# Half-height matmuls for one product of the GNN's first layer, and its bias moved from TensorE to ScalarE

## The chip, the cores and the metric

One core of a Trainium2 chip runs the kernel. The metric is the device time of one execution in microseconds (us), the median over runs. A profile of one further execution shows what each engine did: TensorE (PE, with its weight loads as PEld), VectorE (DVE), ScalarE (ACT), GpSimd (POOL) and SyncE (SP), which issues most DMAs.

## The reference

```
h   = relu(layernorm(x))                        # x: 50000 x 256
agg = mean of edge_attr over the edges by dst   # 25000 x 64 -> 50000 x 64, edges sorted by dst
h1  = relu(concat([agg, h], 1) @ W1 + b1)       # W1: 320 x 512
out = x + (h1 @ W2 + b2)                        # W2: 512 x 256
```

All in fp32.

## The kernel before

**Tiles.** The 50000 rows are worked off in 98 tiles (steps t = 0 to 97) of 512 rows. The hidden width of 512 is cut into CH = 4 chunks m of 128, the output rows of a tile into SUB = 4 groups j of 128. Every fp32 operand X of a matmul is split into a rounded high part X_hi (type fp32r) and the rest X_lo = X - X_hi, and a product is made of three fp32r matmuls: hi by hi, lo by hi, hi by lo.

**Layer 1.** For chunk m, `layer1_nodes` adds six 512-column matmuls into PSUM bank m (two halves c of the node features by three products, lines L795 to L797). `layer1_means` adds two: L804 takes the weights wa_hi (rows of W1 that belong to the means, twice) by QA, whose upper 64 partitions hold the means' high part and whose other 64 hold their low part; L805 takes wb_lo by QB. QB holds the means' high part in partitions 0 to 63 and ones below; wb_lo holds the low weights of the means in partitions 0 to 63 and, in rows 64 and 96, the bias b1 as high and low part against those ones. So L805 does two things with one matmul: the product of the means' high part with the low weights (64 rows), and the bias. Eight matmuls make a chunk, the eighth releases it (s_l1).

**Evictions.** ACT (`hidden_high`, L530) writes H1_hi = relu(bank) as fp32r; then DVE (`hidden_low`, L646) writes H1_lo = max(bank, 0) - H1_hi from the bank and H1_hi.

**Layer 2.** `layer2` makes 16 pairs of a 512-column matmul (L815, H1_hi by both parts of W2) and a 256-column one (L817, H1_lo by W2's high part). Its order is (j0: m0, m1, m2), (j1: m0, m1, m2), (j0: m3), (j1: m3), then j2 and j3 whole. Before each matmul of j0 it waits for H1_lo of that chunk, since the pair needs it. The first six pairs are therefore what TensorE can do between the end of layer 1 and the arrival of H1_lo of chunk 3.

**Order on each engine, written out by hand.**

- TensorE, step t: chunk 0, chunk 1, `edge_means(t+1)` (eight small matmuls of 64 output columns, L784 and L785, that sum edges into the bank PA), chunk 2, chunk 3, layer 2.
- VectorE, step t: H1_lo chunk 0, two statistics, H1_lo chunk 1, two statistics, H1_lo chunk 2, `ends` (L581) and `aggregate` (L589), transpose 0 of tile t+1 (L630), H1_lo chunk 3, transpose 1, the two HT_lo of t+1 (L638), the one-hot matrices of t+2, residual 0 (two instructions), the means' low part of t+1 (`means_low`, L642), residuals 1 to 3.
- ScalarE, step t: H1_hi of chunks 0 to 3, HT_hi of t+1 (two, L516), `means_high(t+1)` (QB L521, QA L523), four layernorm activations of t+2 (HN, L504), E_hi of t+2.
- SP, step t: load of X for t+3, the edge windows of t+3, `move(t+2)` (four DMAs HQ<-HN, L252, once the four layernorm activations are done), the store of t. The transpose of step t+1 reads HQ.

Banks 2 and 3 of layer 1 are also the output banks j = 2 and 3 of layer 2, so layer 1 waits there for residuals of the tile before (s_fin).

Of the kernel before, what the change touches and what calls it, by code (L numbers as in the profile page):

```python
# [20 lines left out]
def past(eng, sem, value):  # L21

    if not isinstance(value, int) or value > 0:
        eng.wait_ge(sem, value)


def build(nc, x, src, dst, edge_attr, w1, b1, w2, b2, out):
    N, D = x.shape
    E, DE = edge_attr.shape
    H = w1.shape[1]  # L30
    CD, CH = D // P, H // P
# [36 lines left out]
    with ExitStack() as ctx:  # L68
        def sb(name, shape, dt=F32):
            return ctx.enter_context(nc.sbuf_tensor(name, shape, dt))  # L70

        def ps(name, shape, dt=F32):
            return ctx.enter_context(nc.psum_tensor(name, shape, dt))

        def sem(name):
            return ctx.enter_context(nc.semaphore(name))


        ident = sb("ident", [P, P])
# [7 lines left out]
        b2_row = sb("b2_row", [P, D])  # L87
        w1_raw = sb("w1_raw", [P, CD, H])
        wa_raw = sb("wa_raw", [P, H])
        b1_raw = sb("b1_raw", [P, H])  # L90
        w2_raw = sb("w2_raw", [P, CH, D])
        w1_hi = sb("w1_hi", [P, CD, H], F32R)
        w1_lo = sb("w1_lo", [P, CD, H], F32R)
        wa_hi = sb("wa_hi", [P, H], F32R)
        wb_lo = sb("wb_lo", [P, H], F32R)
        b1_hi = sb("b1_hi", [P, H], F32R)
        w2_both = sb("w2_both", [P, CH, 2, D], F32R)


# [43 lines left out]
        HT_hi = sb("HT_hi", [P, CD, TILE], F32R)  # L143
        HT_lo = sb("HT_lo", [P, CD, TILE], F32R)
        QA = sb("QA", [P, TILE], F32R)
        QB = sb("QB", [P, TILE], F32R)
        H1_hi = sb("H1_hi", [P, CH, TILE], F32R)
        H1_lo = sb("H1_lo", [P, CH, TILE], F32R)

# [23 lines left out]
        PA = ps("PA", [P, TILE])  # L173
# [177 lines left out]
        @block.gpsimd  # L351
        def _(pool):
            pool.memset(dst_b[:], 1 << 20).then_inc(s_zero, 1)
            pool.memset(b1_raw[:], 0.0).then_inc(s_zero, 1)
            pool.iota(thresholds[:], pattern=[[P, KS], [TILE, TILES]], base=0, channel_multiplier=0,
                      allow_small_or_imprecise_dtypes=True).then_inc(s_zero, 1)
            pool.wait_ge(s_zero, 3)
            pool.iota(thresholds[:, :, TILES - 1:TILES], pattern=[[P, KS], [0, 1]], base=LAST, channel_multiplier=0,
                      allow_small_or_imprecise_dtypes=True).then_inc(s_const, 1)
            pool.memset(ones_bf[:], 1.0).then_inc(s_const, 1)  # L360
# [55 lines left out]
            pool.wait_ge(s_whi, 5)  # L416
# [68 lines left out]
        def _(act):  # L485
# [3 lines left out]
                              w1[DE + q * QF:DE + (q + 1) * QF, :].rearrange("(c f) h -> f c h", f=QP)).then_inc(s_w[0], 16)  # L489
            for a in range(2):  # L490
                act.dma_start(wa_raw[a * DE:(a + 1) * DE, :], w1[0:DE, :]).then_inc(s_w[1], 16)
            act.wait_ge(s_zero, 3)
            for p in (64, 96):
                act.dma_start(b1_raw[p:p + 1, :], b1.rearrange("(o h) -> o h", o=1)).then_inc(s_w[2], 16)
            for a in range(2):
                act.dma_start(w2_raw[:, 2 * a:2 * a + 2, :],
                              w2[2 * a * P:2 * (a + 1) * P, :].rearrange("(c p) d -> p c d", p=P)).then_inc(s_w[3], 16)
# [20 lines left out]
            def means_high(t):  # L518
                past(act, s_l1, CH * t)
                act.wait_ge(s_sum, t + 1)  # L520
                act.activation(QB[0:DE, :], PA[0:DE, :], ACT.Copy).then_inc(s_qhi, 1)  # L521
                act.wait_ge(s_qhi, 2 * t + 1)
                act.activation(QA[0:DE, :], QB[0:DE, :], ACT.Copy).then_inc(s_qhi, 1)  # L523

            def hidden_high(t):
                for m in range(CH):
                    act.wait_ge(s_l1, CH * t + m + 1)
                    if m == 0:
                        past(act, s_l2, SUB * t)
                    act.activation(H1_hi[:, m, :], bank(m)[:], ACT.Relu).then_inc(s_1hi, 1)  # L530

            act.wait_ge(s_w[0], 16 * QN)
            act.activation(w1_hi[:], w1_raw[:], ACT.Copy).then_inc(s_whi, 1)
            act.wait_ge(s_w[1], 32)
            act.activation(wa_hi[:], wa_raw[:], ACT.Copy).then_inc(s_whi, 1)
            act.wait_ge(s_w[2], 32)
            act.activation(b1_hi[DE:P, :], b1_raw[DE:P, :], ACT.Copy).then_inc(s_whi, 1)
            act.activation(wb_lo[64:96, :], b1_raw[64:96, :], ACT.Copy).then_inc(s_whi, 1)
            act.wait_ge(s_w[3], 32)
            act.activation(w2_both[:, :, 0, :], w2_raw[:], ACT.Copy).then_inc(s_whi, 1)  # L540
            layernorm(0, 0)
# [27 lines left out]
        def _(dve):  # L569
# [69 lines left out]

            def means_low(t):  # L640
                dve.wait_ge(s_qhi, 2 * t + 1)
                dve.tensor_tensor(QA[DE:P, :], PA[0:DE, :], QB[0:DE, :], ALU.subtract).then_inc(s_qlo, 1)  # L642

            def hidden_low(t, m):
                dve.wait_ge(s_1hi, CH * t + m + 1)
                dve.scalar_tensor_tensor(out=H1_lo[:, m, :], in0=bank(m)[:], scalar=0.0, in1=H1_hi[:, m, :],  # L646
                                         op0=ALU.max, op1=ALU.subtract).then_inc(s_1lo, 1)

            def residual(t, b, j):
                dve.wait_ge(s_l2, SUB * t + j + 1)  # L650
# [8 lines left out]
            def step(t, b, later=True, latest=True):  # L659
# [22 lines left out]
                for j in range(1, SUB):  # L682
# [13 lines left out]
                                     in1=behind[:, HALO:HALO + ER_], op0=ALU.add, op1=ALU.add).then_inc(s_runs, 1)  # L696
# [6 lines left out]
            with dve.If(flag != 0):  # L703
# [3 lines left out]
                with dve.Fori(0, SLOTS) as i:  # L707
# [40 lines left out]
            ends(0, 0)  # L748
            onehot(0, 0)

            dve.wait_ge(s_whi, 3)
            dve.tensor_tensor(wb_lo[0:DE, :], wa_raw[0:DE, :], wa_hi[0:DE, :], ALU.subtract).then_inc(s_wblo, 1)
            dve.tensor_tensor(wb_lo[96:P, :], b1_raw[96:P, :], b1_hi[96:P, :], ALU.subtract).then_inc(s_wblo, 1)
            means_low(0)
            ends(1, 1)
            onehot(1, 1)
# [10 lines left out]
        def _(pe):  # L767
# [7 lines left out]
            pe.wait_ge(s_const, 13)  # L775

            def edge_means(t, b):
                pe.wait_ge(s_oh, SUB * t + SUB)
# [9 lines left out]
            def layer1_nodes(t, m):  # L788
                if m == 0:
                    pe.wait_ge(s_hlo, 2 * t + 2)  # L790
                if m >= 2:
                    past(pe, s_fin, SUB * (t - 1) + m + 1)
                cols = slice(m * P, (m + 1) * P)
                for c in range(CD):
                    pe.matmul(bank(m)[:], w1_hi[:, c, cols], HT_hi[:, c, :], start=(c == 0), stop=False)  # L795
                    pe.matmul(bank(m)[:], w1_hi[:, c, cols], HT_lo[:, c, :], start=False, stop=False)  # L796
                    pe.matmul(bank(m)[:], w1_lo[:, c, cols], HT_hi[:, c, :], start=False, stop=False)  # L797

            def layer1_means(t, m):
# [78 lines left out]
```

## Time and profile before

| | |
|---|---|
| median of 3 runs | 1381.35 us (1381.05 to 1381.44) |
| the profiled execution | 1381.12 us |
| its span from the first to the last instruction | 1379.1 us |
| mean granted TensorE clock | 0.989 |
| busy: PE, PEld, DVE, ACT, POOL | 1340.5, 1122.1, 1202.3, 696.5, 533.0 us |

A matmul's record lasts from its start to the modelled end of its results, so records of consecutive matmuls overlap; what a matmul costs is the distance from its start to the next one's. Between steps the pattern repeats every 13.54 us.

### The profile page before, as it was taken

The numbers are of one execution on the slowest core, as the hardware profiler recorded it, in microseconds if no ns is written. First come the engines' busy times: TensorE is split into PE (matmuls) and PEld (weight loads), VectorE is DVE, ScalarE is ACT, GpSimd is POOL, SyncE is SP. The second block draws the span as 40 slices with busy tenths as digits, with TensorE's granted clock in tenths as the row PEclk, the third lists the DMA queues.
The fourth block names the chain that finished last, engine by engine and source line by source line (L and its number), as shares of the span: only waits on it lengthen the run. The fifth ranks groups of instructions, "written<-read, shape, count | busy, mean of one in ns | idle before, by whom it ended". The sixth has DMA issues, their size and how long they took to land.

```text
span 1379.1 us, 29845 instructions
## 1 busy us (share of the span) xinstructions
PE 1340.5 (97%) x7078; PEld 1122.1 (81%) x7078; DVE 1202.3 (87%) x2979; ACT 696.5 (51%) x1280; POOL 533.0 (39%) x709
## 2 busy tenths in 40 slices
PE   2799999999999999999999999999999999999998
PEld 0588888888888888888888888888888888888887
DVE  7598989898888989898988888898889898898986
ACT  3354545455554545454555545454545555454543
POOL 4334343433333343434333343434343443434341
PEclk7899999999999999999999999999999999999999
DMA  5567676766767676867667676758676766767672
GB/s 108 89 122 136 115 143 110 138 113 135 116 132 129 119 138 113 143 111 138 114 135 115 133 131 117 133 118 142 109 141 113 136 117 131 120 129 132 118 128 56
DMA packets 424904, 169.49 MB, mean 123 GB/s; under 512 B 323190, under 2 KB 424506, under 8 KB 424892
## 3 DMA queue, kind: packets, MB, share of 16 engines
q1 hardware_dynamic: 421608, 167.40, 67.0%
q10 hardware_dynamic: 3284, 1.97, 0.8%
q14 instruction: 9, 0.07, 0.0%
q8 instruction: 3, 0.05, 0.0%
HBM read 66.50 MB, written 51.40 MB: 85 GB/s over the span
## 4 chain that ended last, share of the span: by engine, by line
PE 96%; DVE 2%; DMA 1%; SPq 1%; issue 0%
PE P L815 26%; PE P L817 14%; PE P L795 13%; PE P L797 13%; PE P L796 13%; PE P L804 7%; PE P L805 7%; PE PA L785 2%; PE PA L784 2%; DVE below L597 1%; DMA X<-in_x_dram 0%; DMA dst_a<-in_dst_dram 0%; SPq L275 0%; DMA table_dram<-table 0%; SPq L276 0%
## 5 line engine op out<-in xcount | busy, mean ns | idle before, releaser
L815 PE MATMUL P<-w_both,H_hi 128*128 128x512 f32 x1568 | 552.1, 393 | 4.7 <-DVE H_lo L646 4.7
L530 ACT ACTIVATE H_hi<-P 128x512 fp32r<-128x512 f32 x392 | 234.6, 599 | 509.9 <-PE P L805 509.9
L817 PE MATMUL P<-w_both,H_lo 128*128 128x256 f32 x1568 | 442.5, 282 | 0.0
L646 DVE SCALAR_TENSOR_TENSOR H_lo<-P,H_hi 128x512 fp32r<-128x512 f32 x392 | 268.8, 686 | 108.4 <-ACT H_hi L530 101.8
L815 PEld LDWEIGHTS P<-w_both,H_hi 128*128 128x128 f32 x1568 | 295.3, 188 | 71.0 <-DVE H_lo L646 6.2
L795 PE MATMUL P<-HT_hi,w_hi 128*128 128x512 f32 x784 | 316.0, 403 | 19.5 <-DVE HT_lo L638 19.5
L797 PE MATMUL P<-HT_hi,w_lo 128*128 128x512 f32 x784 | 310.8, 396 | 0.0
L796 PE MATMUL P<-HT_lo,w_hi 128*128 128x512 f32 x784 | 310.4, 396 | 0.0
L817 PEld LDWEIGHTS P<-w_both,H_lo 128*128 128x128 f32 x1568 | 297.0, 189 | 4.5
L409 POOL TENSOR_TENSOR XB<-X,b_row 128x1024 f32<-128x1024 f32 x98 | 234.9, 2397 | 137.9 <-DVE O L657 137.9
L403 POOL TENSOR_TENSOR E_lo<-ES,E_hi 128x256 fp32r<-128x256 f32 x98 | 73.1, 746 | 416.0 <-ACT E_hi L510 416.0
L630 DVE STREAM_TRANSPOSE HT<-HQ 128x512 f32<-128x512 f32 x196 | 212.9, 1087 | 7.3 <-DMA HQ<-HN 5.7
L504 ACT ACTIVATE HN<-X,shift,rstd 128x256 f32<-128x256 f32 x392 | 202.4, 587 | 10.2 <-POOL shift L392 10.2
L795 PEld LDWEIGHTS P<-HT_hi,w_hi 128*128 128x128 f32 x784 | 148.1, 189 | 49.7 <-issue 19.6
L516 ACT ACTIVATE HT_hi<-HT 128x512 fp32r<-128x512 f32 x196 | 123.9, 633 | 127.2 <-DVE HT L630 127.1
L657 DVE TENSOR_TENSOR O<-P,XB 128x256 f32<-128x256 f32 x392 | 166.5, 425 | 13.4
L797 PEld LDWEIGHTS P<-HT_hi,w_lo 128*128 128x128 f32 x784 | 147.8, 189 | 35.3
L796 PEld LDWEIGHTS P<-HT_lo,w_hi 128*128 128x128 f32 x784 | 148.2, 189 | 26.4
L655 DVE TENSOR_TENSOR XB<-P,XB 128x256 f32<-128x256 f32 x392 | 163.9, 418 | 4.7 <-PE P L817 1.6
L804 PE MATMUL P<-QA,wa_hi 128*128 128x512 f32 x392 | 155.1, 396 | 1.6 <-DVE QA L642 1.6
L805 PE MATMUL P<-QB,wb_lo 128*128 128x512 f32 x392 | 154.1, 393 | 0.0
L638 DVE TENSOR_TENSOR HT_lo<-HT,HT_hi 128x512 fp32r<-128x512 f32 x196 | 134.6, 687 | 17.9 <-ACT HT_hi L516 16.1
(72 smaller groups left out, 1136.9 us busy)
## 6 DMA issues: line engine op xcount, KB each, us to landing
X<-in_x_dram SPq DMA_DIRECT2D x98, 512.0 KB, 4.2
HQ<-HN SPq DMA_DIRECT2D x388, 128.0 KB, 4.2
out_dram<-O SPq DMA_DIRECT2D x97, 512.0 KB, 4.8
ER<-in_edge_attr_dram SPq DMA_DIRECT2D x392, 32.0 KB, 1.8
DT<-table_dram SPq DMA_DIRECT2D x392, 1.0 KB, 1.7
w_raw<-in_L_gnn_W_dram ACTq DMA_DIRECT2D x4, 128.0 KB, 7.2
w_raw<-in_L_gnn_W_dram ACTq DMA_DIRECT2D x2, 256.0 KB, 8.6
HQ<-HN ACTq DMA_DIRECT2D x4, 128.0 KB, 4.1
```

The source lines that it names most:

```text
L409: pool.tensor_tensor(XB[b][:], X[b][:], b2_row[:].unsqueeze(1).to_broadcast([P, SUB, D]), ALU.add).then_inc(s_xb, 1)
L504: act.activation(HN[b][:, j, :], X[b][:, j, :], ACT.Relu, bias=shift[b][:, j:j + 1], scale=rstd[b][:, j:j + 1]).then_inc(s_ln, 1)
L530: act.activation(H1_hi[:, m, :], bank(m)[:], ACT.Relu).then_inc(s_1hi, 1)
L630: dve.transpose(HT[:, c, :].rearrange("p (j n k) -> p k j n", j=SUB, k=QN), HQ[b][:, :, c * QP:(c + 1) * QP].rearrange("p (k j) f -> p k j ...
L646: dve.scalar_tensor_tensor(out=H1_lo[:, m, :], in0=bank(m)[:], scalar=0.0, in1=H1_hi[:, m, :], op0=ALU.max, op1=ALU.subtract).then_inc(s_1 ...
L795: pe.matmul(bank(m)[:], w1_hi[:, c, cols], HT_hi[:, c, :], start=(c == 0), stop=False)
L796: pe.matmul(bank(m)[:], w1_hi[:, c, cols], HT_lo[:, c, :], start=False, stop=False)
L797: pe.matmul(bank(m)[:], w1_lo[:, c, cols], HT_hi[:, c, :], start=False, stop=False)
L804: pe.matmul(bank(m)[:], wa_hi[:, cols], QA[:], start=False, stop=False)
L805: pe.matmul(bank(m)[:], wb_lo[:, cols], QB[:], start=False, stop=True).then_inc(s_l1, 1)
L815: pe.matmul(out_bank(j)[:], H1_hi[:, m, rows], w2_both[:, m, :, :].rearrange("p a d -> p (a d)"), start=(m == 0), stop=False)
L817: last = pe.matmul(out_bank(j)[:, 0:D], H1_lo[:, m, rows], w2_both[:, m, 0, :], start=False, stop=(m == CH - 1))
```

## The change

The bias leaves the matmuls. The product of the means' high part with the low weights becomes matmuls of 64 rows: the one for chunk m reads partitions 0 to 63 (QA, wb_lo), the one for chunk m+1 reads partitions 64 to 127 (QC, a second copy of the high part, and the second copy of the low weights in wb_lo). The two follow each other at the head of chunks 0 and 2 and write different banks. `layer1_means` keeps one matmul per chunk. ScalarE adds the bias, now a column b1_col per chunk, in two evictions of each chunk: H1_hi in fp32r as before, and H1 in fp32. VectorE subtracts the two, both from SBUF, instead of reading the bank.

```
-        b1_raw = sb("b1_raw", [P, H])
+        b1_col = sb("b1_col", [P, CH])
-        QB = sb("QB", [P, TILE], F32R)
+        QC = sb("QC", [P, TILE], F32R)
+        H1 = sb("H1", [P, CH, TILE])
 # gpsimd: memsets of b1_raw and of QB's ones are gone
 # scalar, start
-            act.wait_ge(s_zero, 3)
-            for p in (64, 96):
-                act.dma_start(b1_raw[p:p + 1, :], b1.rearrange("(o h) -> o h", o=1)).then_inc(s_w[2], 16)
+            act.dma_start(b1_col[:], b1.rearrange("(m p) -> p m", p=P),
+                          allow_slow_non_contiguous=True).then_inc(s_w[2], 16)
-            act.activation(b1_hi[DE:P, :], b1_raw[DE:P, :], ACT.Copy).then_inc(s_whi, 1)
-            act.activation(wb_lo[64:96, :], b1_raw[64:96, :], ACT.Copy).then_inc(s_whi, 1)
 # scalar, means_high
-                act.activation(QB[0:DE, :], PA[0:DE, :], ACT.Copy).then_inc(s_qhi, 1)
+                act.activation(QA[0:DE, :], PA[0:DE, :], ACT.Copy).then_inc(s_qhi, 1)
                 act.wait_ge(s_qhi, 2 * t + 1)
-                act.activation(QA[0:DE, :], QB[0:DE, :], ACT.Copy).then_inc(s_qhi, 1)
+                act.activation(QC[DE:P, :], QA[0:DE, :], ACT.Copy).then_inc(s_qhi, 1)
 # scalar, hidden_high
-                    act.activation(H1_hi[:, m, :], bank(m)[:], ACT.Relu).then_inc(s_1hi, 1)
+                    act.activation(H1_hi[:, m, :], bank(m)[:], ACT.Relu, bias=b1_col[:, m:m + 1]).then_inc(s_1hi, 1)
+                    act.activation(H1[:, m, :], bank(m)[:], ACT.Relu, bias=b1_col[:, m:m + 1]).then_inc(s_1, 1)
 # vector
-                dve.tensor_tensor(QA[DE:P, :], PA[0:DE, :], QB[0:DE, :], ALU.subtract).then_inc(s_qlo, 1)
+                dve.tensor_tensor(QA[DE:P, :], PA[0:DE, :], QA[0:DE, :], ALU.subtract).then_inc(s_qlo, 1)
                 dve.wait_ge(s_1hi, CH * t + m + 1)
-                dve.scalar_tensor_tensor(out=H1_lo[:, m, :], in0=bank(m)[:], scalar=0.0, in1=H1_hi[:, m, :],
-                                         op0=ALU.max, op1=ALU.subtract).then_inc(s_1lo, 1)
+                dve.wait_ge(s_1, CH * t + m + 1)
+                dve.tensor_tensor(H1_lo[:, m, :], H1[:, m, :], H1_hi[:, m, :], ALU.subtract).then_inc(s_1lo, 1)
 # tensor
-                if m >= 2:
-                    past(pe, s_fin, SUB * (t - 1) + m + 1)
+            def layer1_pair(t, m):
+                first = not (isinstance(t, int) and t == 0)
+                if m == 0:
+                    pe.wait_ge(s_qhi, 2 * t + 2)
+                else:
+                    past(pe, s_fin, SUB * t)
+                pe.matmul(bank(m)[:], wb_lo[0:DE, m * P:(m + 1) * P], QA[0:DE, :], start=first, stop=False)
+                pe.matmul(bank(m + 1)[:], wb_lo[DE:P, (m + 1) * P:(m + 2) * P], QC[DE:P, :], start=first, stop=False)
 # tensor, layer1_means
-                pe.matmul(bank(m)[:], wa_hi[:, cols], QA[:], start=False, stop=False)
-                pe.matmul(bank(m)[:], wb_lo[:, cols], QB[:], start=False, stop=True).then_inc(s_l1, 1)
+                pe.matmul(bank(m)[:], wa_hi[:, m * P:(m + 1) * P], QA[:], start=False, stop=True).then_inc(s_l1, 1)
 # tensor, step
                 for m in range(CH):
+                    if m % 2 == 0:
+                        layer1_pair(t, m)
                     if not (isinstance(t, int) and t == 0):
                         layer1_nodes(t, m)
                     layer1_means(t, m)
```

## Rows read from the trace of the kernel before

**Rows 1.** The page's head, and its part on busy time.

```profile
span 1379.1 us, 29845 instructions
...
PE 1340.5 (97%) x7078; PEld 1122.1 (81%) x7078; DVE 1202.3 (87%) x2979; ACT 696.5 (51%) x1280; POOL 533.0 (39%) x709
```

**Rows 2.** The page's chain that ended last, by engine.

```profile
PE 96%; DVE 2%; DMA 1%; SPq 1%; issue 0%
```

**Rows 3.** The page's groups: the two evictions' lines.

```profile
L530 ACT ACTIVATE H_hi<-P 128x512 fp32r<-128x512 f32 x392 | 234.6, 599 | 509.9 <-PE P L805 509.9
...
L646 DVE SCALAR_TENSOR_TENSOR H_lo<-P,H_hi 128x512 fp32r<-128x512 f32 x392 | 268.8, 686 | 108.4 <-ACT H_hi L530 101.8
```

**Rows 4.** Timeline, one step, TensorE: start, length, engine, line, operation.

```profile
702.03 0.22 PE L785 MATMUL PA<-OH,E_lo 128*64 128x128 f32 x1
702.03 0.19 PEld L795 LDWEIGHTS P<-HT_hi,w_hi 128*128 128x128 f32 x1
702.09 0.45 PE L795 MATMUL P<-HT_hi,w_hi 128*128 128x512 f32 x1
...
702.37 0.40 PE L796 MATMUL P<-HT_lo,w_hi 128*128 128x512 f32 x1
...
703.77 0.39 PE L805 MATMUL P<-QB,wb_lo 128*128 128x512 f32 x1
...
705.86 0.40 PE L815 MATMUL P<-w_both,H_hi 128*128 128x512 f32 x1
...
706.10 0.28 PE L817 MATMUL P<-w_both,H_lo 128*128 128x256 f32 x1
...
707.96 0.39 PE L815 MATMUL P<-w_both,H_hi 128*128 128x512 f32 x1
...
711.31 0.28 PE L817 MATMUL P<-w_both,H_lo 128*128 128x256 f32 x1
...
711.43 0.40 PE L795 MATMUL P<-HT_hi,w_hi 128*128 128x512 f32 x1
```

**Rows 5.** Timeline, the same step, ScalarE, VectorE and SP's queue.

```profile
701.10 0.69 DVE L646 SCALAR_TENSOR_TENSOR H_lo<-P,H_hi 128x512 fp32r<-128x512 f32 x1
...
704.20 0.60 ACT L530 ACTIVATE H_hi<-P 128x512 fp32r<-128x512 f32 x1 [1.79 <-PE P L805]
...
704.82 0.69 DVE L646 SCALAR_TENSOR_TENSOR H_lo<-P,H_hi 128x512 fp32r<-128x512 f32 x1 [1.03 <-ACT H_hi L530]
...
705.81 1.11 DVE L630 STREAM_TRANSPOSE HT<-HQ 128x512 f32<-128x512 f32 x1
...
706.75 0.68 DVE L646 SCALAR_TENSOR_TENSOR H_lo<-P,H_hi 128x512 fp32r<-128x512 f32 x1
...
709.62 0.63 ACT L523 ACTIVATE QA<-QB 64x512 fp32r<-64x512 f32 x1
...
710.16 2.07 ACT L504 ACTIVATE HN<-X,shift,rstd 128x256 f32<-128x256 f32 x4
...
712.25 2.73 SPq L252 DMA_DIRECT2D HQ<-HN  x4
```

**Rows 6.** Timeline, first step: two evictions in a row, and X's arrival.

```profile
45.83 1.06 ACT L530 ACTIVATE H_hi<-P 128x512 fp32r<-128x512 f32 x2
...
52.45 0.75 DVE L575 BATCH_NORM_STATS2 stats<-X 128x6 f32<-128x256 f32 x2 [5.32 <-DMA X<-in_x_dram]
```

**Rows 7.** Timeline, a later step in which TensorE waited inside layer 2.

```profile
883.39 0.67 DVE L646 SCALAR_TENSOR_TENSOR H_lo<-P,H_hi 128x512 fp32r<-128x512 f32 x1
...
883.86 0.28 PE L817 MATMUL P<-w_both,H_lo 128*128 128x256 f32 x1
...
884.11 0.51 PE L815 MATMUL P<-w_both,H_hi 128*128 128x512 f32 x1
...
884.45 0.28 PE L817 MATMUL P<-w_both,H_lo 128*128 128x256 f32 x1
```

**Rows 8.** The tile HQ, whole run: waits for it (us, times); its DMAs.

```profile
  DMA HQ<-HN: 5.7, 23
...
DMA to landing us min/median/max: 3.3/4.2/5.4
```

More of the change, by code:

```diff
@@ L95, in build @@
         wb_lo = sb("wb_lo", [P, H], F32R)
-        b1_hi = sb("b1_hi", [P, H], F32R)
         w2_both = sb("w2_both", [P, CH, 2, D], F32R)
@@ L226, in build @@
         s_1hi = sem("s_1hi")
+        s_1 = sem("s_1")
         s_1lo = sem("s_1lo")
@@ L353, in _ @@
             pool.memset(dst_b[:], 1 << 20).then_inc(s_zero, 1)
-            pool.memset(b1_raw[:], 0.0).then_inc(s_zero, 1)
             pool.iota(thresholds[:], pattern=[[P, KS], [TILE, TILES]], base=0, channel_multiplier=0,
                       allow_small_or_imprecise_dtypes=True).then_inc(s_zero, 1)
-            pool.wait_ge(s_zero, 3)
+            pool.wait_ge(s_zero, 2)
             pool.iota(thresholds[:, :, TILES - 1:TILES], pattern=[[P, KS], [0, 1]], base=LAST, channel_multiplier=0,
@@ L375, in _ @@
             pool.wait_ge(s_const, 10)
-            pool.memset(QB[DE:P, :].bitcast(F32), 1.0).then_inc(s_const, 1)
+            pool.memset(ident[:], 0.0).then_inc(s_const, 1)
             pool.wait_ge(s_const, 11)
-            pool.memset(ident[:], 0.0).then_inc(s_const, 1)
-            pool.wait_ge(s_const, 12)
             pool.affine_select(out=ident[:], in_=ident[:], compare_op=ALU.not_equal, fill=1.0, base=0,
@@ L415, in _ @@
             pool.tensor_tensor(w1_lo[:], w1_raw[:], w1_hi[:], ALU.subtract).then_inc(s_wlo, 1)
-            pool.wait_ge(s_whi, 5)
+            pool.wait_ge(s_whi, 3)
             pool.tensor_tensor(w2_both[:, :, 1, :], w2_raw[:], w2_both[:, :, 0, :], ALU.subtract).then_inc(s_wlo, 1)
@@ L535, in _ @@
             act.activation(wa_hi[:], wa_raw[:], ACT.Copy).then_inc(s_whi, 1)
-            act.wait_ge(s_w[2], 32)
-            act.activation(b1_hi[DE:P, :], b1_raw[DE:P, :], ACT.Copy).then_inc(s_whi, 1)
-            act.activation(wb_lo[64:96, :], b1_raw[64:96, :], ACT.Copy).then_inc(s_whi, 1)
+            act.wait_ge(s_w[2], 16)
             act.wait_ge(s_w[3], 32)
@@ L749, in _ @@
             onehot(0, 0)
-            dve.wait_ge(s_whi, 3)
-            dve.tensor_tensor(wb_lo[0:DE, :], wa_raw[0:DE, :], wa_hi[0:DE, :], ALU.subtract).then_inc(s_wblo, 1)
-            dve.tensor_tensor(wb_lo[96:P, :], b1_raw[96:P, :], b1_hi[96:P, :], ALU.subtract).then_inc(s_wblo, 1)
+            dve.wait_ge(s_whi, 2)
+            dve.tensor_tensor(wb_lo[:], wa_raw[:], wa_hi[:], ALU.subtract).then_inc(s_wblo, 1)
             means_low(0)
@@ L774, in _ @@
             pe.matmul(PA[0:1, 0:1], ones_f[0:EP, :], fall[:], start=True, stop=True).then_inc(s_found, 1)
-            pe.wait_ge(s_const, 13)
+            pe.wait_ge(s_const, 12)
             def edge_means(t, b):
@@ L790, in layer1_nodes @@
                     pe.wait_ge(s_hlo, 2 * t + 2)
-                if m >= 2:
-                    past(pe, s_fin, SUB * (t - 1) + m + 1)
                 cols = slice(m * P, (m + 1) * P)
                 for c in range(CD):
-                    pe.matmul(bank(m)[:], w1_hi[:, c, cols], HT_hi[:, c, :], start=(c == 0), stop=False)
+                    pe.matmul(bank(m)[:], w1_hi[:, c, cols], HT_hi[:, c, :],
+                              start=(c == 0 and isinstance(t, int) and t == 0), stop=False)
                     pe.matmul(bank(m)[:], w1_hi[:, c, cols], HT_lo[:, c, :], start=False, stop=False)
                     pe.matmul(bank(m)[:], w1_lo[:, c, cols], HT_hi[:, c, :], start=False, stop=False)
+            def layer1_pair(t, m):
[6 more added lines that the diff above has]
+                pe.matmul(bank(m + 1)[:], wb_lo[DE:P, (m + 1) * P:(m + 2) * P], QC[DE:P, :], start=first, stop=False)
             def layer1_means(t, m):
@@ L801, in layer1_means @@
                     pe.wait_ge(s_qlo, t + 1)
-                    pe.wait_ge(s_qhi, 2 * t + 2)
-                cols = slice(m * P, (m + 1) * P)
-                pe.matmul(bank(m)[:], wa_hi[:, cols], QA[:], start=False, stop=False)
-                pe.matmul(bank(m)[:], wb_lo[:, cols], QB[:], start=False, stop=True).then_inc(s_l1, 1)
+                pe.matmul(bank(m)[:], wa_hi[:, m * P:(m + 1) * P], QA[:], start=False, stop=True).then_inc(s_l1, 1)
             def layer2(t):
@@ L846, in _ @@
             pe.wait_ge(s_wlo, 2)
-            pe.wait_ge(s_wblo, 2)
-            pe.wait_ge(s_whi, 5)
+            pe.wait_ge(s_wblo, 1)
+            pe.wait_ge(s_whi, 3)
             step(0, 0)
```

## The prediction

> **What bounds the kernel now.** I read the page's busy times first, then the chain that ended last, then one step of the timeline. TensorE is busy for 97% of the span and is 96% of the chain [rows 1, 2]; VectorE follows with 87%, ScalarE is at 51%. A share doesn't tell whether TensorE could go faster, so the timeline of one step matters. There the first L795 of a step starts 13.54 us after the one before (the pattern's period), and the matmuls stand without a gap: six pairs of layer 2 take 707.96 - 705.86 = 2.10 us, 0.35 each, of which the 512-column matmul is 0.233 (705.86 to 706.10) and the 256-column one 0.116 [rows 4]. So a period is 32 layer-1 matmuls x 0.233 = 7.45, plus 16 x 0.35 = 5.58, plus about 0.5 for the eight edge matmuls: TensorE is filled. Any matmul taken out is worth its 0.233 us, as long as nothing else comes due. The rest of this prediction is about what comes due.
>
> The nearest thing is H1_lo of chunk 3. The seventh L815 (707.96) needs it; DVE ended it at 706.75 + 0.68 = 707.43 [rows 4, 5]. The slack is 0.53 us.
>
> **The change, part by part.** All times below are per step, in us.
>
> *Taken out:* four full L805, 4 x 0.233 = 0.93.
>
> *Added on TensorE:* two pairs of 64-row matmuls of 512 columns. No row shows a 64-row matmul. The bounds: if the two run at the same time, a pair costs one matmul, 0.24; if they run one after the other, 0.466; either may have a cost of switching on top. Between them lies the weight load. Both pairs stand behind a short matmul: the first behind a 256-column L817, the second behind the last 128-column L785 [rows 4]. A load starts when the matmul before starts; after the last L785 the load of L795 started at 702.03, and the next matmul came at 702.37 and not 0.233 after 702.09, so the full load took until about 702.14, or 0.11. If the second load of a pair can't go together with the first, the second matmul starts 0.11 late and a pair costs 0.35. I take 0.24: the halves use different partitions, different weights and different banks, so nothing that I see has to be shared. TensorE's work is then 13.54 - 0.93 + 0.48 = 13.09.
>
> The Trainium skill, page "TensorE: Matmul & The Clock Gate", Part 3 (The mechanism), has such matmuls start some 4 ns apart, with the loads pulled ahead; that would make a pair 0.24, and the sum above stands at it. No row here shows it.
>
> *Added on ScalarE:* a second eviction per chunk. Two evictions in a row took 1.06 together, so the second starts 0.46 after the first and ends 1.06 after the first's start [rows 6]; a bias from another address should not change this. ScalarE has 509.9 us of idle time before its evictions [rows 3], over five a step, and takes four times 0.46 = 1.84 more: not a bound. But the low part now waits for the second eviction: it comes 0.46 later behind its chunk.
>
> *VectorE:* subtracts from SBUF and no longer from the bank. I take the same 0.69 as for L646 [rows 3]; no gain, no loss.
>
> *The new wait.* Let S be the start of the last matmul of chunk 2 (703.77, L805). Before: eviction at S + 0.43, H1_lo of chunk 2 at S + 1.05, transpose 0 at 705.81, which is 0.99 behind it, H1_lo of chunk 3 at 706.75, another 0.94, and its end 0.68 later: S + 3.66 [rows 4, 5]. The eviction of chunk 3 is not what this waits for; VectorE's order is. After: everything from H1_lo of chunk 2 on is 0.46 later, so its chunk 3 ends at S + 4.12. TensorE gets there sooner: chunk 3 has seven matmuls instead of eight, so the seventh L815 comes due at S + 0.233 x 8 + 2.10 = S + 3.96 (before S + 4.19). It is late by 0.16. On top comes what a wait costs when it happens: in the one example H1_lo ended at 883.39 + 0.67 = 884.06, the L815 was recorded at 884.11, and the L817 behind it came 0.34 after that and not 0.233, because its weight load was no longer hidden [rows 7]. So 0.16 after the end of H1_lo the matmul really runs. The stall is 0.16 + 0.16 = 0.32.
>
> *What is late behind it.* Transpose 1, HT_hi, the means, the layernorm and the HQ moves hang on transpose 0 and shift along. Between transpose 0 and the end of the layernorm activations lie 712.23 - 705.81 = 6.42; from there to the next transpose 0 there are 13.54 - 6.42 = 7.12 for four DMAs, whose last is issued some 2.1 after and landed up to 5.4 later [rows 5, 8]. Today this wait occurs 23 times for 5.7 us in all, and mostly disappears in the slack of 0.53. With a period near 13.41 the room shrinks by 0.13, and there is no slack in front of TensorE any more: (5.7 + 23 x 0.13) / 97 = 0.09; I take 0.08.
>
> *Things that I cost at nothing.* The pair needs QC at the head of the step: the copy ended at 709.62 + 0.63 = 710.25 [rows 5], 5.43 behind H1_lo of chunk 2. In the new step, counted from the start of its first pair, S is at 0.24 + 14 x 0.233 + 0.53 + 0.24 + 6 x 0.233 = 5.67, that H1_lo at 7.18, QC at 12.6, and the next pair at 13.4: 0.8 to spare. The pair of chunk 2 waits for all four residuals of the step before instead of three: these were done when the next step's first H1_lo started, 701.10 + 13.54 - 704.82 = 9.82 behind that of chunk 2, so at 17.0, and the pair comes at 13.4 + 4.0 = 17.4: 0.4 to spare. If either cover went, TensorE would stall by the excess in every step. The start (bias load, two activations, a subtraction and two memsets fewer) ends in any case with the wait for X until 52.45 [rows 6].
>
> *Sum.* 13.09 + 0.32 + 0.08 = 13.49, against 13.54. 96 steps save 0.05, 4.8 us, and the last step, which has no transpose in front of its H1_lo, saves the full 0.45. 1381.12 - 5.2 = 1375.9. The profiled execution is 0.2 below the median of 1381.35, so I say 1376. Of 44 us that TensorE's own work gives up (97 x 0.45), nearly all is eaten by the later low part.
>
> **The rivals.**
>
> *A, my forecast (chance 0.45):* pairs at 0.24. 1376; with the stall 0.1 smaller or larger it is 1366 to 1386.
>
> *B, the second weight load shows (0.25):* a pair is 0.35, TensorE's work 13.31, with the stall 0.32 and a little HQ wait (0.03) 13.66, 0.12 more than now: 1392. Slower. It decides from the point where the pair exceeds 0.27. For it: both pairs stand behind short matmuls [rows 4]. Against it: the loads use different rows.
>
> *C, no side by side at all (0.15):* four matmuls of 0.233 as before, so only the later low part counts: 13.54 + 0.32 + 0.03 = 13.89, 0.35 more: 1381 + 34 = 1415. For it: no row shows two matmuls at once.
>
> *D, the array empties at each change of height (0.10):* a matmul's record is 0.39 long and the next starts after 0.233 [rows 4], so emptying costs up to 0.16; four changes per step are 0.64. 13.49 + 0.64 - 0.05 = 14.08: 1381 + 52 = 1433. Against it: the change to the edge matmuls' 64 columns and back costs only 0.05 (702.09 to 702.37 is 0.28) [rows 4].
>
> The Trainium skill, page "TensorEngine Tiling (Array Packing)", Key Properties, has a change of tiling mode drain TensorE; that is this case. The 0.05 around the edge matmuls, a change of columns, speaks against it; a change of rows no run has shown so far.
>
> *E, the stall doesn't come (0.05):* were H1_lo of chunk 3 on time, only TensorE's work would count: 13.09, 97 x 0.45 = 44 less, 1338. The 0.16 by which it is late leaves little room for that.
>
> **How the numbers follow.** The likeliest is A, 1376, with 1366 to 1386 of its own. The range leaves out D and the depth of E: 1364 to 1416. What tells a change from none here is 0.2%, 2.8 us: below 1378.6 lies some two thirds of A and all of E, 0.36; between 1378.6 and 1384.1 some of A and a bit of B, 0.14; above, the rest of A, B, C and D, 0.50.
>
> **What would show it.** The two L-lines of the pair should start a few ns apart, and the matmul behind them 0.24 after the first (B: 0.35; C: 0.47). Before the seventh L815 of a step there should be idle time ended by H1_lo, some 0.2 us by the record, in nearly every step, and the L817 behind it at 0.34. ScalarE should be near 64% to 65% busy. DVE's idle time before H1_lo, now 108.4 us, should rise, and the waits for HQ be more than 23. I am wrong if pairs don't overlap, if a bias from a table of its own makes the eviction longer, or if the subtraction from SBUF takes another time than that from PSUM.

## The result, and the profile after

The changed kernel takes 1490.34 us (median of 4 runs, 1490.01 to 1491.79) against 1381.39 us before: a ratio of 1.0788 (95% interval 1.0773 to 1.0803). It is 109 us slower. The forecast was 1376 us with a range of 1364 to 1416; even the worst rival, 1433, was too fast.

The page of the changed kernel: span, busy times, the chain by engine, and the groups of the evictions and of GpSimd's addition.

```profile
span 1487.1 us, 30480 instructions
...
PE 1419.4 (95%) x7078; PEld 1089.3 (73%) x7078; DVE 1388.1 (93%) x2978; ACT 967.1 (65%) x1670; POOL 531.6 (36%) x707
...
PE 51%; DVE 21%; issue 19%; ACT 5%; DVEq 2%; SPq 1%; DMA 1%; POOL 0%; POOLq 0%
...
L643 DVE TENSOR_TENSOR H_lo<-H,H_hi 128x512 fp32r<-128x512 f32 x392 | 466.8, 1191 | 38.9 <-ACT H L528 38.9
L527 ACT ACTIVATE H_hi<-P,b_col 128x512 fp32r<-128x512 f32 x392 | 269.7, 688 | 299.8 <-PE P L806 299.8
...
L407 POOL TENSOR_TENSOR XB<-X,b_row 128x1024 f32<-128x1024 f32 x98 | 234.4, 2391 | 125.5 <-DVE O L653 125.5
L528 ACT ACTIVATE H<-P,b_col 128x512 f32<-128x512 f32 x392 | 267.2, 682 | 0.0
```

Against [rows 1 to 3]: TensorE was 96% of the chain and is 51%; VectorE's busy time grew by 186 us though it runs one instruction fewer. One group explains it: H1_lo takes 1191 ns on average instead of 686, 198 us more in all. An average hides what happens, so the timeline of one step, VectorE and GpSimd (and the two matmuls that wait):

```profile
710.56 2.39 POOL L407 TENSOR_TENSOR XB<-X,b_row 128x1024 f32<-128x1024 f32 x1 [1.31 <-DVE O L653]
710.66 2.84 DVE L643 TENSOR_TENSOR H_lo<-H,H_hi 128x512 fp32r<-128x512 f32 x1 [0.26 <-ACT H L528]
...
715.34 0.67 DVE L643 TENSOR_TENSOR H_lo<-H,H_hi 128x512 fp32r<-128x512 f32 x1
...
715.67 0.28 PE L818 MATMUL P<-w_both,H_lo 128*128 128x256 f32 x1
716.07 0.50 PE L816 MATMUL P<-w_both,H_hi 128*128 128x512 f32 x1
...
717.20 0.68 DVE L643 TENSOR_TENSOR H_lo<-H,H_hi 128x512 fp32r<-128x512 f32 x1
...
717.93 0.50 PE L816 MATMUL P<-w_both,H_hi 128*128 128x512 f32 x1 [0.21 <-DVE H_lo L643]
```

Three of the four H1_lo of a step take 0.67 us. The first takes 2.84: it starts 0.10 us after GpSimd's addition, and it ends 0.55 us after the addition has ended (712.95). It was held up for the whole addition. The addition starts when the last residual of the step before is done, and H1_lo of chunk 0 is VectorE's next instruction after that residual, so the two meet in every step.

TensorE feels this at a place that the prediction did not look at. After the hold-up all of VectorE's work is late, and H1_lo of chunk 2 ends at 715.34 + 0.67 = 716.01. The third L816 of layer 2, which needs it, starts at 716.07, 0.40 us after the L818 ahead of it and not 0.12. The second wait, before the seventh L816 (717.93), is the one that was forecast.

The same step on TensorE, around the first pair:

```profile
706.72 0.28 PE L818 MATMUL P<-w_both,H_lo 128*128 128x256 f32 x1
706.93 0.49 PE L800 MATMUL P<-QA,wb_lo 64*128 64x512 f32 x1
706.93 0.50 PE L801 MATMUL P<-QC,wb_lo 64*128 64x512 f32 x1
707.36 0.50 PE L788 MATMUL P<-HT_hi,w_hi 128*128 128x512 f32 x1
707.70 0.40 PE L790 MATMUL P<-HT_lo,w_hi 128*128 128x512 f32 x1
...
721.60 0.49 PE L800 MATMUL P<-QA,wb_lo 64*128 64x512 f32 x1
```

The two halves do start together. Height means here the number of rows (partitions) that a matmul reads, 64 or 128. The 256-column matmul ahead of them takes 0.21 instead of 0.12 [rows 4], the pair 0.43 instead of 0.23, and the full-height matmul behind it 0.34 instead of 0.23. From 706.72 to 707.70 there are 0.98 us where the two full-height neighbours alone take 0.35: a pair costs 0.63. The period is 721.60 - 706.93 = 14.67, before 13.54.

The weight loads show the other half of the price. In a stream of full-height matmuls the load starts ahead of its matmul (702.03 for the one at 702.09 in [rows 4]). Here neither does:

```profile
706.93 0.18 PEld L800 LDWEIGHTS P<-QA,wb_lo 64*128 64x128 f32 x1 [0.24 <-issue]
...
707.36 0.19 PEld L788 LDWEIGHTS P<-HT_hi,w_hi 128*128 128x128 f32 x1 [0.24 <-issue]
```

### The profile page after: what moved, and what is told of

It is laid out like the page before. It is cut to its first block, busy times and chain, and to the rows that moved or that the text cites. A ratio compares the mean times of both kernels' runs of the same rounds, so it can differ in the third digit from the quotient of the medians.

```text
span 1487.1 us, 30480 instructions
## 1 busy us (share of the span) xinstructions
PE 1419.4 (95%) x7078; PEld 1089.3 (73%) x7078; DVE 1388.1 (93%) x2978; ACT 967.1 (65%) x1670; POOL 531.6 (36%) x707
## 4 chain that ended last, share of the span: by engine, by line
PE 51%; DVE 21%; issue 19%; ACT 5%; DVEq 2%; SPq 1%; DMA 1%; POOL 0%; POOLq 0%
PE P L816 17%; DVE H_lo L643 9%; PE P L818 8%; PE P L788 8%; DVE stats L571 7%; PE P L790 6%; PE P L791 6%; ACT H L528 4%; PE P L806 3%; PE P L800 3%; DVE mv L585 2%; DVE HT L626 2%; DMA dst_w<-in_dst_dram 1%; DVE rel L577 1%; DVEq L24 0%
## 5 line engine op out<-in xcount | busy, mean ns | idle before, releaser
L816 PE MATMUL P<-w_both,H_hi 128*128 128x512 f32 x1568 | 580.7, 406 | 33.7 <-DVE H_lo L643 23.1
L643 DVE TENSOR_TENSOR H_lo<-H,H_hi 128x512 fp32r<-128x512 f32 x392 | 466.8, 1191 | 38.9 <-ACT H L528 38.9
L527 ACT ACTIVATE H_hi<-P,b_col 128x512 fp32r<-128x512 f32 x392 | 269.7, 688 | 299.8 <-PE P L806 299.8
L818 PE MATMUL P<-w_both,H_lo 128*128 128x256 f32 x1568 | 441.1, 281 | 0.0
L816 PEld LDWEIGHTS P<-w_both,H_hi 128*128 128x128 f32 x1568 | 294.8, 188 | 153.7 <-DVE H_lo L643 96.2
L788 PE MATMUL P<-HT_hi,w_hi 128*128 128x512 f32 x784 | 330.7, 422 | 19.5 <-DVE HT_lo L634 19.5
L818 PEld LDWEIGHTS P<-w_both,H_lo 128*128 128x128 f32 x1568 | 296.9, 189 | 4.6
L528 ACT ACTIVATE H<-P,b_col 128x512 f32<-128x512 f32 x392 | 267.2, 682 | 0.0
```

The source lines that it names most:

```text
L527: act.activation(H1_hi[:, m, :], bank(m)[:], ACT.Relu, bias=b1_col[:, m:m + 1]).then_inc(s_1hi, 1)
L528: act.activation(H1[:, m, :], bank(m)[:], ACT.Relu, bias=b1_col[:, m:m + 1]).then_inc(s_1, 1)
L643: dve.tensor_tensor(H1_lo[:, m, :], H1[:, m, :], H1_hi[:, m, :], ALU.subtract).then_inc(s_1lo, 1)
L816: pe.matmul(out_bank(j)[:], H1_hi[:, m, rows], w2_both[:, m, :, :].rearrange("p a d -> p (a d)"), start=(m == 0), stop=False)
L818: last = pe.matmul(out_bank(j)[:, 0:D], H1_lo[:, m, rows], w2_both[:, m, 0, :], start=False, stop=(m == CH - 1))
```

## The experiments

Three theories had to be kept apart. P: GpSimd's addition holds up a subtraction whose inputs are both in SBUF. H: the change of height costs TensorE. S: the low part comes later because it stands behind two evictions, with the bias operand as a share of that. The rival to each is that another of them is the whole loss.

**The pairs alone.** The changed kernel with the evictions of before; b1 is left out.

```
-  act.activation(H1_hi[:, m, :], bank(m)[:], ACT.Relu, bias=b1_col[:, m:m + 1]).then_inc(s_1hi, 1)
-  act.activation(H1[:, m, :], bank(m)[:], ACT.Relu, bias=b1_col[:, m:m + 1]).then_inc(s_1, 1)
+  act.activation(H1_hi[:, m, :], bank(m)[:], ACT.Relu).then_inc(s_1hi, 1)
-  dve.tensor_tensor(H1_lo[:, m, :], H1[:, m, :], H1_hi[:, m, :], ALU.subtract)...
+  dve.scalar_tensor_tensor(out=H1_lo[:, m, :], in0=bank(m)[:], scalar=0.0, in1=H1_hi[:, m, :], ...)
```

> The changed kernel's matmuls with the evictions of before (H1_lo from the bank, one eviction per chunk); the bias b1 is left out. Theory P (the loss is VectorE, held up while GpSimd's 2.4 us addition reads SBUF, because H1_lo now takes both inputs from SBUF; the pairs cost some 0.3 us per step by themselves): every H1_lo back at 0.69 us, TensorE full again with a period of 13.54 - 0.93 + 2 x 0.61 = 13.83, so about 1409 us. Rival H (the pairs with their changes of height are the loss): near 1490 us.

1406.24 us, ratio 1.0176 (1.0159 to 1.0193), 3 us from P's number. H1_lo is back at 0.685 us on average. The pairs by themselves cost 25 us, 0.26 per step. The two pairs of the changed kernel (0.63 above, 0.58 for the one behind the edge matmuls) less the 0.93 taken out give 0.28.

**The evictions alone.** The kernel before, with H1 written by a second eviction (no bias operand, the bias stays in L805) and the subtraction from SBUF.

> The kernel before with only its evictions changed: the bias stays in the full-height matmul, ScalarE evicts each chunk twice (no bias operand), VectorE subtracts from SBUF. Theory P: VectorE sets the pace as in the changed kernel, one H1_lo per step takes 2.8 us, about 1480 us. Rival H: only the later low part counts, at most 0.1 us per step, about 1390 us.

1442.88 us, ratio 1.0445 (1.0428 to 1.0462): between the two. Two steps on the timeline, VectorE and GpSimd:

```profile
718.37 0.68 DVE L650 TENSOR_TENSOR H_lo<-H,H_hi 128x512 fp32r<-128x512 f32 x1
...
720.01 1.85 DVE L650 TENSOR_TENSOR H_lo<-H,H_hi 128x512 fp32r<-128x512 f32 x1 [0.29 <-ACT H L533]
...
732.43 2.85 DVE L650 TENSOR_TENSOR H_lo<-H,H_hi 128x512 fp32r<-128x512 f32 x1 [0.26 <-issue]
```

```profile
718.62 2.69 POOL L411 TENSOR_TENSOR XB<-X,b_row 128x1024 f32<-128x1024 f32 x1 [1.44 <-DVE O L660]
732.33 2.39 POOL L411 TENSOR_TENSOR XB<-X,b_row 128x1024 f32<-128x1024 f32 x1 [1.44 <-DVE O L660]
```

In the first step VectorE starts first: its H1_lo takes 0.68 and GpSimd's addition 2.69, that is, GpSimd waits. But the addition then still runs when H1_lo of chunk 1 comes, and holds that one up for its rest (1.85). In the second step GpSimd starts 0.10 earlier: it takes its 2.39 and VectorE's H1_lo of chunk 0 2.85. Whoever is first holds the other. The two kinds of step alternate; over the run 50 of the H1_lo of chunk 0 are short and 48 long. A long step lasts 14.66 on average and a short one 13.72, because less of the hold-up reaches TensorE. In the changed kernel nearly all are long; there H1_lo of chunk 0 waits for its second eviction ([0.26 <-ACT H L528] above) and so comes behind the addition. H1_lo averages 1084 ns here. P's 1480 took VectorE to set the pace; it doesn't, TensorE waits for single low parts.

The Trainium skill, page "SBUF — State Buffer", section "Who interferes with whom", says just this: a VectorE instruction with two SBUF inputs contends with a GpSimd instruction that reads SBUF, and the one that issues first has the shared ports for its whole instruction. The two steps above agree with it; it was not weighed in the prediction.

**GpSimd reads nothing.** The changed kernel (without X and b2 in the output) with `pool.memset(XB[b][:], 0.0)` for the addition, behind a tiny addition of 4 columns that carries its waits.

> The changed kernel, with GpSimd's addition XB = X + b2 put in the place of a memset of XB, which reads nothing from SBUF; the output lacks X and b2. Theory P: no H1_lo takes longer than 0.7 us; the period falls from 14.67 to what TensorE needs, 13.83, plus a wait of about 0.5 for the low part of chunk 3, 14.3, so about 1457 us. If the time doesn't move, P is wrong.

1468.14 us, ratio 1.0625 (1.0608 to 1.0643). No H1_lo is over 0.7 us. So P is right about the block and wrong about its size: 22 us of 109. Relieved of it, VectorE is at 82% and TensorE waits for the low part of chunk 3, period 14.43. A write that takes 0.95 us beside an H1_lo holds nobody up. The memset is also shorter than the addition, so the run doesn't say whether reading or length mattered; no run here has a write as long as the addition.

**Full height instead of pairs.** The changed kernel with four matmuls of 128 rows; the upper half of QC holds zeros.

```
-  pe.matmul(bank(m)[:], wb_lo[0:DE, m * P:(m + 1) * P], QA[0:DE, :], start=first, stop=False)
-  pe.matmul(bank(m + 1)[:], wb_lo[DE:P, (m + 1) * P:(m + 2) * P], QC[DE:P, :], start=first, stop=False)
+  for n in (m, m + 1):
+      pe.matmul(bank(n)[:], wb_lo[:, n * P:(n + 1) * P], QC[:], start=first, stop=False)
```

> The changed kernel with four full-height matmuls in the place of the two pairs (QC's upper half holds zeros, so the result is the same product). TensorE's own work falls by the cost of the changes of height, some 0.3 us per step. Theory P (VectorE sets the pace): no change, 1490 us within 5. Rival H (TensorE sets it): 1490 - 97 x 0.29 = 1462 us.

1461.17 us, ratio 1.0576 (1.0558 to 1.0593). The rival was right: four full matmuls in place of two pairs save 29 us. That VectorE alone sets the pace was wrong. H1_lo falls to 1094 ns, since in every other step VectorE now starts first and H1_lo of chunk 1 is held up in its place (1.9 us). That hardly shows in TensorE's waits, though: they add up to 0.83 per step here and to 0.84 in the changed kernel (table below). Of the 0.29 by which the period falls, 0.28 is what TensorE spent on the pairs.

**The addition in four parts.** The changed kernel, `pool.tensor_tensor` over 256 columns four times.

> The changed kernel, GpSimd's addition XB = X + b2 cut into four instructions of 256 columns. Theory L (the engine that starts first keeps the other from SBUF for the length of one instruction): the first H1_lo of a step waits for at most one of the four, 0.6 us, and takes at most 1.3 us instead of 2.8; VectorE no longer sets the pace and the time falls to that of the run in which GpSimd only writes, about 1468 us. Rival M (the block lasts until GpSimd has nothing left to do): H1_lo stays at 2.8 us and the time at 1490.

1464.12 us, ratio 1.0603 (1.0586 to 1.0621). The first H1_lo of a step and the first three parts:

```profile
713.71 1.04 DVE L644 TENSOR_TENSOR H_lo<-H,H_hi 128x512 fp32r<-128x512 f32 x1 [0.41 <-ACT H L529]
```

```profile
713.47 3.13 POOL L408 TENSOR_TENSOR XB<-X,b_row 128x256 f32<-128x256 f32 x3 [1.29 <-DVE O L654]
```

GpSimd still reads all of X here, so what is gone is the length of one instruction. VectorE gets in after the first part, which takes 0.73, and GpSimd waits in its turn: the second and third part take 1.19 and 1.30. The block lasts for one instruction, and L holds: 26 us less. The time is even 4 us under that of the run without reads. There the matmuls of layer 2 stand slightly further apart (0.06 per step in all); why is open.

**No bias operand.** The run without reads, with both evictions without `bias=b1_col[...]`; b1, b2 and X are left out.

> As the run in which GpSimd only writes XB (1468 us, period 14.44), but both evictions without the bias operand, so b1 is left out too. The evictions with the operand take 0.69 us at a distance of 0.59, without it 0.60 and 0.50. Theory S (TensorE waits for the low part, which comes after both evictions): the low part comes 0.18 us sooner, the period falls to about 14.26, 1451 us. Rival: the wait is set by VectorE's own work, and the time stays at 1468.

1447.78 us, ratio 1.0482 (1.0464 to 1.0499). The first two lines are of the run without reads, the next fence of this one, ScalarE in chunk 2:

```profile
707.01 0.69 ACT L528 ACTIVATE H_hi<-P,b_col 128x512 fp32r<-128x512 f32 x1 [1.47 <-PE P L807]
707.60 0.68 ACT L529 ACTIVATE H<-P,b_col 128x512 f32<-128x512 f32 x1
```

```profile
709.28 0.60 ACT L528 ACTIVATE H_hi<-P 128x512 fp32r<-128x512 f32 x1 [1.65 <-PE P L807]
709.77 0.59 ACT L529 ACTIVATE H<-P 128x512 f32<-128x512 f32 x1
```

With b1_col as an operand an eviction takes 0.09 us longer, and two of them end 0.19 us later. TensorE waits for that: 20 us less, 0.19 per step of the period, of which 0.10 is at the seventh pair of layer 2 and 0.07 at the third. S holds. The Trainium skill, page "ScalarE: Activation LUTs", section "What ACT_TABLE_LOAD costs", gives some 93 ns for each per-partition operand of an activation; the 0.69 against 0.60 agrees.

**No side by side.** The pairs-only kernel (b1 left out), both matmuls of a pair on partitions 0 to 63.

> As the run with the pairs only (1406 us), but both matmuls of a pair read partitions 0 to 63, so that they can't lie side by side. Theory C (the two halves do run at the same time, the loss of a pair is the change of height before and after it): each pair 0.23 us longer, 1406 + 97 x 0.47 = 1451 us. Rival N (they took turns all along): 1406 us.

1449.49 us, ratio 1.0491 (1.0474 to 1.0509). One pair, behind the edge matmuls:

```profile
708.17 0.49 PE L799 MATMUL P<-QA,wb_lo 64*128 64x512 f32 x1
708.50 0.39 PE L800 MATMUL P<-QA,wb_lo 64*128 64x512 f32 x1
708.82 0.50 PE L787 MATMUL P<-HT_hi,w_hi 128*128 128x512 f32 x1
```

43 us more than with the halves apart, 0.22 per pair: two halves on different partitions really run at the same time. Each pair writes two different banks in both runs.

**Pairs together.** The pairs-only kernel with all four 64-row matmuls at the head of chunk 2.

```
-                    if m % 2 == 0:
+                    if m == 2:
                         layer1_pair(t, m)
+                for n in (0, 2):
+                    pe.matmul(bank(2)[:], wb_lo[0:DE, n * P:(n + 1) * P], QA[0:DE, :], ...)
+                    pe.matmul(bank(3)[:], wb_lo[DE:P, (n + 1) * P:(n + 2) * P], QC[DE:P, :], ...)
```

> As the run with the pairs only (1406 us), but both pairs stand together at the head of chunk 2 (those of chunks 0 and 1 go into the banks of chunks 2 and 3, so the sums are not the reference's). Theory C (a change of height costs about 0.2 us each, the matmuls themselves 0.23 per pair): two changes fewer per step, some 0.37 us, 1406 - 36 = 1370 us. Rival: the cost belongs to each 64-row matmul, 1406 us.

1367.59 us, ratio 0.9903 (0.9886 to 0.9919), faster than before.

```profile
708.93 0.49 PE L798 MATMUL P<-QA,wb_lo 64*128 64x512 f32 x1
708.93 0.50 PE L799 MATMUL P<-QC,wb_lo 64*128 64x512 f32 x1
709.26 0.39 PE L798 MATMUL P<-QA,wb_lo 64*128 64x512 f32 x1
709.27 0.39 PE L799 MATMUL P<-QC,wb_lo 64*128 64x512 f32 x1
709.59 0.50 PE L787 MATMUL P<-HT_hi,w_hi 128*128 128x512 f32 x1
```

The two changes that fell away were worth 38.7 us, 0.40 per step, so 0.20 each. The cost belongs to the change of height, not to the 64-row matmul. The timeline has it in two halves: at a change the last matmul ahead lasts 0.09 to 0.10 longer, and the first matmul behind 0.10 longer, because its weight load starts with it and not ahead of it. A lone pair has both (0.43 = 0.23 + 0.10 + 0.10); here the first pair has one and the second the other (0.33 each). Together the four 64-row matmuls cost 0.79 per step in this form (0.93 less the 0.14 by which the period fell), as two lone pairs 1.19, as full-height matmuls 0.93.

**A version with the whole reference.** The pairs together between edge_means and chunk 2, one eviction with the bias operand, and the low part from the bank. VectorE can't add the bias, take the maximum and subtract in one instruction; but max(z, -b) = relu(z + b) - b, so it makes the low part minus b, and b times W2's high part goes once into b2.

```
+  act.activation(H1_hi[:, m, :], bank(m)[:], ACT.Relu, bias=b1_col[:, m:m + 1]).then_inc(s_1hi, 1)
+  dve.scalar_tensor_tensor(out=H1_lo[:, m, :], in0=bank(m)[:], scalar=nb1_col[:, m:m + 1],
+                           in1=H1_hi[:, m, :], op0=ALU.max, op1=ALU.subtract).then_inc(s_1lo, 1)
+  # once: PS = b1 (broadcast) x W2_hi, b2_sum = PS + b2
+  # tensor, step: nodes and means of chunks 0 and 1; edge_means(t+1); all four 64-row matmuls; chunks 2 and 3
+  # vector, step: the four statistics, H1_lo 0 and 1, aggregate, ends, H1_lo 2, transpose 0, ...
```

> A version that computes the whole reference. Both pairs stand together between edge_means and chunk 2, where those of chunks 0 and 1 close their banks; one eviction per chunk with the bias operand; VectorE takes max(bank, -b1) - H1_hi from the bank, which is the low part minus b1, and b1 times W2's high part is added once to b2 at the start; its statistics come ahead of the first H1_lo. Theory C with L and S (changes of height cost 0.2 us each, no block by GpSimd, no second eviction): the period of the grouped run, 13.40, and so 1367 to 1371 us, faster than before by 0.8%. Rival: the evictions of chunks 0 and 1 now come in a bunch and push those of chunk 2 and 3, TensorE waits for the low part again, 1380 us or more.

1381.43 us, ratio 0.9996 (0.9987 to 1.0005): no gain. The rival's number came, but not by its mechanism: what comes late is transpose 0, which waits for its DMA. The group of the transposes:

```profile
L631 DVE STREAM_TRANSPOSE HT<-HQ 128x512 f32<-128x512 f32 x196 | 213.1, 1088 | 35.7 <-DMA HQ<-HN 34.4 <-issue 1.3
```

34.4 us of waits for HQ against 5.7 [rows 8]. This is the loop of the prediction (transpose 0, layernorm, moves of HQ, next transpose 0), which leaves no room at a period under 13.54. H1_lo of chunk 3 stands behind transpose 0 on VectorE, and TensorE waits for it:

```profile
721.43 1.11 DVE L631 STREAM_TRANSPOSE HT<-HQ 128x512 f32<-128x512 f32 x1 [0.38 <-DMA HQ<-HN]
722.39 0.68 DVE L647 SCALAR_TENSOR_TENSOR H_lo<-P,nb_col,H_hi 128x512 fp32r<-128x512 f32 x1
...
723.12 0.50 PE L828 MATMUL P<-w_both,H_hi 128*128 128x512 f32 x1
```

That is nearly all of the 0.11 by which the period (13.52) lies above the grouped run's 13.40. The start is also some 2 us later.

**The loop shortened, and a control.** Two of the four layernorm activations go between the two HT_hi, where ScalarE is idle (the preparations of b1 go to ScalarE too, and the first tile keeps VectorE's old order). The control is the kernel before with the moved activations alone.

```
                 for c in range(CD):
                     ...
+                    if c == 0 and between is not None:
+                        layernorm(*between, js=(0, 1))
```

> The version before this one (1381 us, period 13.52, 95 waits for HQ of 34 us in all, and a start 2.4 us later than that of the kernel before), with two of the four layernorm activations moved between the two HT_hi, where ScalarE is idle, so that the moves of HQ go out about 0.9 us sooner; the first tile keeps VectorE's old order, and the small preparations of b1 are ScalarE's. Theory Q (the loop transpose 0, layernorm, moves of HQ, next transpose 0 set that period): nearly no waits for HQ, period 13.40, 1368 us, 1% below before. Rival R (the bunched evictions set it): 1379 us or more.

> Control: the kernel before with the same move of two layernorm activations and nothing else. TensorE is full there and the waits for HQ (5.7 us in all) disappear in slack, so nothing should change: 1381 us, at most 1 us less. If this alone gave the gain, the gain of the version above would not be that of the grouped pairs.

1371.25 us, ratio 0.9923 (0.9909 to 0.9936), and for the control 1380.87 us, ratio 0.9995 (0.9985 to 1.0005). The group again, and the first two matmuls of two steps:

```profile
L635 DVE STREAM_TRANSPOSE HT<-HQ 128x512 f32<-128x512 f32 x196 | 213.4, 1089 | 1.3 <-issue 1.3
```

```profile
708.46 0.40 PE L805 MATMUL P<-HT_hi,w_hi 128*128 128x512 f32 x1
...
721.87 0.40 PE L805 MATMUL P<-HT_hi,w_hi 128*128 128x512 f32 x1
```

The waits for HQ are gone and the period is that of the grouped run (13.40 on average in both). The control shows that the moved activations give nothing by themselves. What is missing to 1368 must then lie outside the steady steps; at the start, layer 2 of the first tile goes on at 58.28 us (53.84 us in the kernel before).

## Why the prediction was wrong

The 109 us divide along a line of runs: before 1381.4; pairs 1406.2 (+25); second eviction and subtraction from SBUF, with neither operand nor reads by GpSimd, 1447.8 (+42); bias operand 1468.1 (+20); GpSimd's reads 1490.3 (+22). Per step that is 0.26 + 0.43 + 0.21 + 0.23 = 1.13.

The distances between the starts of TensorE's matmuls say where each share lies. In us per step over the kernel before, means of the 92 steady steps of each profile:

| run | layer 1 and the way into it (the pairs) | at the third pair of layer 2 (low part of chunk 2) | at the seventh (low part of chunk 3) | rest | period |
|---|---|---|---|---|---|
| before | 0 | 0 | 0 | 0 | 13.54 |
| pairs alone | 0.28 | -0.01 | -0.01 | -0.01 | 13.80 |
| evictions alone | 0 | 0.31 | 0.32 | 0.01 | 14.18 |
| no reads, no operand | 0.28 | 0 | 0.36 | 0.05 | 14.23 |
| no reads | 0.28 | 0.08 | 0.47 | 0.07 | 14.43 |
| addition in four | 0.28 | 0.09 | 0.46 | 0.01 | 14.38 |
| full height | 0 | 0.36 | 0.47 | 0.01 | 14.37 |
| changed kernel | 0.28 | 0.38 | 0.47 | 0 | 14.66 |

The block by GpSimd is the difference between the last row and the addition in four: 0.28, all of it at the third pair. It makes VectorE 2.17 us longer (2.84 - 0.67), and most of that falls into time that VectorE had idle. The forecast had TensorE's waits at the seventh pair alone, and its own work 0.45 shorter; in fact that grew by 0.28.

- *"I take 0.24"* for a pair: wrong, 0.63 and 0.58, the largest error of the sum (0.73 per step). The two do lie side by side, as A said; the price is of changing the height, 0.20 each time, as rival D had it. D's 0.16 per change was the tail of a matmul's record; measured are 0.09 to 0.10 of waiting ahead of the change and 0.10 of a weight load that isn't hidden behind it, so D was close in part by luck. D stood at a chance of 0.10, because the edge matmuls' change of columns costs 0.05 [rows 4]. That row was no witness for a change of rows. The Trainium skill, page "TensorEngine Tiling (Array Packing)", Key Properties, has a change of tiling mode drain TensorE; the 0.21 and 0.43 above agree.
- *"no gain, no loss"* for the subtraction from SBUF: the step that failed worst in kind. I took a duration from instructions that never met GpSimd's addition. It would have taken one question more: which of GpSimd's instructions runs beside it? In [rows 5] H1_lo of chunk 0 starts at 701.10, and the addition is the next line:

```profile
701.20 2.40 POOL L409 TENSOR_TENSOR XB<-X,b_row 128x1024 f32<-128x1024 f32 x1 [1.44 <-DVE O L657]
```

  That H1_lo reads the bank and takes its 0.69. The trace of before even holds a meeting of two such instructions, in the first step:

```profile
38.95 1.34 POOL L403 TENSOR_TENSOR E_lo<-ES,E_hi 128x256 fp32r<-128x256 f32 x1 [0.53 <-ACT E_hi L510]
...
39.01 0.68 DVE L752 TENSOR_TENSOR wb_lo<-wa_raw,wa_hi 64x512 fp32r<-64x512 f32 x1
...
39.72 1.12 DVE L753 TENSOR_TENSOR wb_lo<-b_raw,b_hi 32x512 fp32r<-32x512 f32 x1
```

  L403 mostly takes 0.74, and 1.34 here: L752 holds it up, though L403 has the earlier start on record, by 0.06. L753 is as wide as L752, starts while L403 still runs, and takes 1.12. In the changed kernel, where GpSimd's recorded start is 0.09 or more ahead, VectorE waits; a lead of 0.06 did not decide it here.
- *"a bias from another address should not change this"*: wrong, 0.09 us per eviction, 20 us in all. The prediction named it as a way to be wrong and gave it no price. Its figure for ScalarE, 64% to 65% busy, came true by luck: longer evictions in a longer span.
- *The new wait, 0.32:* the mechanism was right and the size nearly so: 0.36 with the same eviction lengths as assumed (the second eviction starts 0.49 after the first in the steady state, and not the 0.46 of [rows 6]). The other 0.07 of that run's 0.43 is not this wait: layer 2's matmuls stand a little further apart, as in the run without reads.
- *HQ, 0.08:* never came due in the changed kernel, whose period is longer. It came due in the version built on it, where it cost 0.11 of the 0.14 per step that the grouping gained.
- *The start* costs nothing, as said.

With D's price TensorE's own work would have been 13.73 (13.09 + 0.64); 13.80 was measured. But each rival was priced with all other terms as in the forecast. B, C and D ended at 1433 at most, since none of them contained a second loss.

What stays open: whether the block alone, with nothing else changed, would cost the kernel before anything; no run has it by itself. Whether a long write by GpSimd would hold VectorE up as a read does was not run either. And why layer 2's matmuls stand further apart, 0.05 to 0.07 per step in all, in the two runs without reads is not known.

## What to carry to other kernels

Before an operand moves from PSUM to SBUF, look at what GpSimd runs at that moment: a subtraction with both inputs in SBUF that starts behind a GpSimd addition waits for the whole of it, and cutting GpSimd's instruction into four removed the loss. Price the delay at every instruction that waits for the chain behind it, not only at the last. Half-height matmuls paid here only in a group: count the changes of height (0.20 us each), not the matmuls. When TensorE is shortened, compute the length of the next loop (here 13.5 us around the layernorm and its DMAs) before expecting the gain.

## What the runs showed of the hardware

Two 64-row matmuls on different partitions and banks start at the same time (706.93 both) and cost 0.43 between full-height neighbours; on the same partitions they cost 0.33 + 0.32, 0.22 more. A change between 128 and 64 rows costs 0.20 us, a change between 128 and 64 columns 0.05 for both ways together. ScalarE's eviction of 128x512 takes 0.69 us with the bias column as operand and 0.60 without. VectorE's max and subtract from the bank with such a column as scalar takes 0.75 us (median) against 0.69. A VectorE subtraction with both inputs in SBUF (0.67) takes 2.84 beside a GpSimd addition of 2.39 that started 0.10 before it, and 1.04 where the addition is cut in four. A GpSimd memset (0.95) beside VectorE's subtraction holds up neither.
